# Three of the first eight bursts on bare weights, their sums masked at eviction; fewer ones loaded; the bias added ahead of the sums

## The reference, cut to what matters

```python
x: (128, 128, 512)   cond_8 = y: (128, 8)   weight: (8, 512, 512)   mask: (512, 512)   bias: (512,)
masked_w = weight * mask[None, :, :]
w_bot = einsum('bg,got->bot', y, masked_w)          # one 512x512 matrix per batch entry
out   = x + einsum('bnt,bot->bno', x, w_bot) + bias
```

## Time and profile before

| | |
|---|---|
| median of 3 runs | 605.12 us (604.96 to 605.41) |
| the profiled execution | 605.46 us, its span 603.7 us |
| PE busy | 592.5 us (98%) |
| DVE, ACT, POOL busy | 313.5, 142.0, 37.8 us |
| HBM traffic | 245 GB/s over the span, 406 GB/s in the slice from 15 to 30 us |

### The profile page before, as it was taken

One profiled execution on the slowest core, in us unless ns is written; L12 is line 12 of the kernel. 1 busy time (PEld: TensorE's weight loads), 2 busy tenths in 40 slices (PEclk: granted clock), 3 DMA queues, 4 the chain that ended last, 5 costly groups with the idle time before them and its releaser, 6 DMA issues.

```text
span 603.7 us, 14813 instructions
## 1 busy us (share of the span) xinstructions
PE 592.5 (98%) x6343; PEld 515.9 (85%) x6343; DVE 313.5 (52%) x524; ACT 142.0 (24%) x277; POOL 37.8 (6%) x34
## 2 busy tenths in 40 slices
PE   7899999999999999999999999999999999999998
PEld 6899988888888888888888888888888888888886
DVE  3565535455555555464465465555555555654342
ACT  4443322222222222222222222222222222220000
POOL 3430000000000113221000000000000000000000
PEclk9999999999999999999999999999999999999999
DMA  9976656686776899998766756766767766777952
GB/s 325 406 294 184 207 180 208 219 249 217 239 246 214 290 332 354 343 337 288 238 225 224 250 204 239 249 210 231 246 216 230 234 234 228 227 244 242 298 158 87
DMA packets 61089, 148.59 MB, mean 246 GB/s; under 512 B 6880, under 2 KB 9696, under 8 KB 61024
## 3 DMA queue, kind: packets, MB, share of 16 engines
q1 hardware_dynamic: 40176, 113.00, 57.3%
q10 hardware_dynamic: 20848, 34.64, 15.2%
HBM read 114.07 MB, written 33.55 MB: 245 GB/s over the span
## 4 chain that ended last, share of the span: by engine, by line
PE 95%; DMA 2%; DVE 1%; issue 1%; ACTq 0%; ACT 0%; DVEq 0%
PE ps L438 75%; PE ps L415 20%; DMA bias_sb<-in_bias 1%; DMA xs<-in_mask 1%; DVE wbot L321 0%; DVE staged L335 0%; PE ps L398 0%; ACTq L268 0%; DVE staged L349 0%; ACT wbot L263 0%; DVE wm L189 0%; DVE staged L354 0%; ACTq L277 0%; DVEq L161 0%; DVEq L346 0%
## 5 line engine op out<-in xcount | busy, mean ns | idle before, releaser
L438 PE MATMUL ps<-wbot,xs 128*128 128x256 f32 (+1 forms) x2176 | 459.3, 370 | 4.4 <-DVE wbot L321 3.7
L438 PEld LDWEIGHTS ps<-wbot,xs 128*128 128x128 f32 x2176 | 389.7, 190 | 59.2 <-issue 6.3
L321 DVE COPY wbot<-ps 128x512 f32<-128x512 f32 (+1 forms) x272 | 164.1, 649 | 183.8 <-PE ps L438 174.6
L263 ACT ACTIVATE wbot<-ps 128x512 f32<-128x512 f32 (+1 forms) x276 | 140.7, 568 | 400.7 <-PE ps L415 198.1
L415 PEld LDWEIGHTS ps<-y_sb,wm 32*128 32x128 f32 x4096 | 124.9, 190 | 21.7 <-issue 20.6
L415 PE MATMUL ps<-y_sb,wm 32*128 32x128 f32 x4096 | 137.5, 280 | 2.5 <-DVE wm L189 2.0
L349 DVE TENSOR_TENSOR staged<-ps,staged 128x512 f32<-128x512 f32 x111 | 76.3, 687 | 79.8 <-PE ps L438 79.8
L335 DVE TENSOR_TENSOR staged<-staged,bias_sb 128x512 f32<-128x512 f32 x112 | 76.4, 682 | 0.0
L189 POOL TENSOR_TENSOR wm<-wm,mask_sb 128x512 f32<-128x512 f32 x16 | 20.0, 1270 | 216.3 <-DMA mask_sb<-in_mask 216.3
L349 DVE TENSOR_TENSOR staged<-ps,bias_sb 128x256 f32<-128x256 f32 (+1 forms) x24 | 12.2, 510 | 15.5 <-PE ps L438 11.0
L189 POOL TENSOR_TENSOR wm<-wm,xs 128x512 f32<-128x512 f32 x14 | 17.6, 1274 | 21.7 <-DMA xs<-in_mask 21.4
(11 more groups left out here) (1 smaller groups left out, 0.1 us busy)
## 6 DMA issues: line engine op xcount, KB each, us to landing
xs<-in_x SPq DMA_DIRECT2D x128, 512.0 KB, 3.9
out<-staged ACTq DMA_DIRECT2D x119, 256.0 KB, 4.7
staged<-in_xn SPq DMA_DIRECT2D x112, 256.0 KB, 4.3
wm<-in_w SPq DMA_DIRECT2D x12, 512.0 KB, 6.4
mask_sb<-in_mask SPq DMA_DIRECT2D x8, 512.0 KB, 6.5
out<-staged ACTq DMA_DIRECT2D x18, 128.0 KB, 4.2
wm<-in_w SPq DMA_DIRECT2D x8, 256.0 KB, 6.8
xs<-in_mask SPq DMA_DIRECT2D x4, 512.0 KB, 13.4
```

The lines of the kernel that those rows point to most:

```text
L263: eng.activation(tile_place(b, j, first, end), tile_sums(b, j, first, end), ACT.Copy).then_inc(s_ev_a, 1)
L321: eng.tensor_copy(tile_place(b, j, first, end), tile_sums(b, j, first, end)).then_inc(s_ev_v, 1)
L438: ins = eng.matmul(bank[:, at_h:at_h + width], xs[:, n % XRING, h, k, :], at, start=(k == 0), stop=(k == KT - 1))
```

## The change

Bursts 0, 2 and 4 (`BARE`) are run on the weights as they come, without mask. VectorE evicts all four strips of them and multiplies by the mask on the way, from a transposed mask `mask_t` (204 KB with a small identity `one_sb`, loaded into the place of mask 0). GpSimd then adds the identity to their sums in `wbot` (`add_one`, one 128x512 instruction for each). Bursts 1, 3 and 5 are evicted by ScalarE alone. `AHEAD` loses 1, 3 and 5. GpSimd multiplies all masks, in the order 1, 3, add_one(0), 5, add_one(2), 6, 7, add_one(4), 8 to 15, and last 0, 2, 4, whose masks are loaded late, behind x 7 and x 9; the later windows need them. `load_x(2)` now also waits for the three add_one. Mask 1 moves to ScalarE's queue. `eye_sb` and `ones_sb` become one tile, blanked by GpSimd and filled by four DMAs of 9 KB that bring only its 16 used partitions. In VectorE's loop `add_bias_to_x(m + 2)` moves ahead of `add_sums(m)`.

```diff
-AHEAD = {1, 3, 5, 7, 8, 10, 12, 14}
+AHEAD = {7, 8, 10, 12, 14}
+BARE = (0, 2, 4)
+MASKED = tuple(_c for _c in range(CS) if _c not in BARE) + BARE
 def on_vector(b, j):
-    return j == 3 or j == 1 and b >= BY_VECTOR
+    if b < BARE[-1] + 2:
+        return b in BARE
+    return j % 2 == 1
...
         def masked(eng, s, c):
-            if s == 0 and c < BY_VECTOR:
-                eng.wait_ge(s_mul_v, c + 1)
-            else:
-                eng.wait_ge(s_mul_p, s * CS + c + 1 - BY_VECTOR)
+            eng.wait_ge(s_mul, len(MASKED) + c + 1 if s else MASKED.index(c) + 1)
...
-                elif c:
+                elif c > 1 and c not in BARE:
                     eng.dma_start(first_mask[:, c:c + count, :], mask[s, :, c:c + count, :]).then_inc(s_mask[c], 16)
             def load_x(n):
...
                     masked(eng, 0, n * 2 - 3)
+                    if n == 2:
+                        eng.wait_ge(s_one, len(BARE))
...
-            for n in range(7, XRING):
-                load_x(n)
+            load_x(7)
+            load_late(0)
+            load_late(1)
+            load_x(8)
+            load_x(9)
+            load_late(2)
...
-            eng.dma_start(first_mask[:, 0, :], mask[0, :, 0, :]).then_inc(s_mask[0], 16)
-            eng.dma_start(eye_sb[:, :, :].rearrange("p v t -> p (v t)").bitcast(fp32), eye).then_inc(s_eye, 16)
-            eng.dma_start(ones_sb[:, :].bitcast(fp32), ones).then_inc(s_eye, 16)
+            eng.dma_start(first_mask[:, 0, 0:KT * GB * BT + BT // 2], mask_t).then_inc(s_mask_t, 16)
+            eng.dma_start(first_mask[:, 1, :], mask[0, :, 1, :]).then_inc(s_mask[1], 16)
+            eng.wait_ge(s_blank, 1)
+            for j in range(TILES):
+                eng.dma_start(eye_sb[j * TR:j * TR + TO, :, :].rearrange("p v t -> p (v t)").bitcast(fp32),
+                              eye[j]).then_inc(s_eye, 16)
...
+            def add_one(b):
+                at = sums[:, b, :, 0, :, :]
+                o = BARE.index(b) * CO
+                eng.wait_ge(s_ev_v, DONE[b, TILES - 1, GROUPS])
+                eng.tensor_tensor(at, at, one_sb[:, o:o + CO].unsqueeze(1).unsqueeze(1).to_broadcast([P, GROUPS, GB, CO]),
+                                  ALU.add).then_inc(s_one, 1)
+
+            for c in MASKED:
+                multiply_mask(eng, 0, c).then_inc(s_mul, 1)
+                if c - 3 in BARE:
+                    add_one(c - 3)
...
+                        if b in BARE:
+                            o = BARE.index(b) * CO + j * TO
+                            by = mask_t_sb[:, :, o:o + TO].unsqueeze(2).to_broadcast([P, KT * GB, GROUPS, TO])
+                            if b == BARE[0]:
+                                eng.wait_ge(s_mask_t, 16)
+                            eng.tensor_tensor(tile_place(b, j, first, end), tile_sums(b, j, first, end), by,
+                                              ALU.mult).then_inc(s_ev_v, 1)
...
-                add_sums(m)
                 if OWN_X <= m + 2 <= LAST:
                     add_bias_to_x(m + 2)
+                add_sums(m)
```

More of the change, by code:

```diff
@@ L99, with cond_resid_kernel @@
 LOAD_W_AT = {LAST_UNIT - GROUPS + 14 + _c: _c for _c in range(0, CS, 2)}
-def cond_resid_kernel(nc: bass.Bass, x, xn, w, mask, bias, yblk, eye, ones, out):
+def cond_resid_kernel(nc: bass.Bass, x, xn, w, mask, mask_t, bias, yblk, eye, out):
     fp32 = mybir.dt.float32
@@ L141, in cond_resid_kernel @@
         s_mask = [sem(f"s_mask{i}") for i in range(CS)]
-        s_mul_v = sem("s_mul_v")
-        s_mul_p = sem("s_mul_p")
+        s_mul = sem("s_mul")
+        s_mask_t = sem("s_mask_t")
+        s_one = sem("s_one")
+        s_late = [sem(f"s_late{c}") for c in BARE]
         s_x = [sem(f"s_x{i}") for i in range(XRING)]
@@ L186, in multiply_mask @@
             eng.wait_ge(s_w[lead], 16 * (s + 1))
-            eng.wait_ge(s_mask[lead], 16 * (s + 1))
-            by = first_mask[:, c, :] if s == 0 else mask_sb[:, c % MASKN, :]
+            if s == 0 and c in BARE:
+                eng.wait_ge(s_late[BARE.index(c)], 16)
+                eng.wait_ge(s_s1, (c + 1) * TILES)
+                by = mask_sb[:, BARE.index(c) % MASKN, :]
+            else:
+                eng.wait_ge(s_mask[lead], 16 * (1 if lead in BARE else s + 1))
+                by = first_mask[:, c, :] if s == 0 else mask_sb[:, c % MASKN, :]
             return eng.tensor_tensor(wm[:, c, :], wm[:, c, :], by, ALU.mult)
@@ L211, in load_w @@
                 if s:
-                    if c >= MASKN:
-                        masked(eng, s, c - 1)
+                    masked(eng, *((s, c - 1) if c >= MASKN else (s - 1, MASKED[-1])))
                     eng.dma_start(mask_sb[:, 0:count, :], mask[s, :, c:c + count, :]).then_inc(s_mask[c], 16)
-                elif c:
+                elif c > 1 and c not in BARE:
                     eng.dma_start(first_mask[:, c:c + count, :], mask[s, :, c:c + count, :]).then_inc(s_mask[c], 16)
@@ L222, in load_x, with load_late @@
                     masked(eng, 0, n * 2 - 3)
+                    if n == 2:
+                        eng.wait_ge(s_one, len(BARE))
                 u, g = divmod(n, GROUPS)
                 eng.dma_start(xs[:, n % XRING, :, :, :], x[u % WINDOWS * GROUPS + g]).then_inc(s_x[n % XRING], 16)
+            def load_late(i):
+                if i >= MASKN:
+                    masked(eng, 0, BARE[i - MASKN])
+                eng.dma_start(mask_sb[:, i % MASKN, :], mask[0, :, BARE[i], :]).then_inc(s_late[i], 16)
             def load_xn(m):
@@ L309, in _ @@
         def _(eng):
-            for s in range(SLICES):
+            eng.memset(eye_sb[:, :, :].rearrange("p v t -> p (v t)").bitcast(fp32), 0.0).then_inc(s_blank, 1)
+            def add_one(b):
[8 more added lines that the diff above has]
+                    add_one(c - 3)
+            for s in range(1, SLICES):
                 for c in range(CS):
-                    if s or c >= BY_VECTOR:
-                        multiply_mask(eng, s, c).then_inc(s_mul_p, 1)
+                    multiply_mask(eng, s, c).then_inc(s_mul, 1)
         @block.vector
@@ L320, in evict @@
                         tile_ready(eng, b, j)
-                        eng.tensor_copy(tile_place(b, j, first, end), tile_sums(b, j, first, end)).then_inc(s_ev_v, 1)
+                        if b in BARE:
[5 more added lines that the diff above has]
+                                              ALU.mult).then_inc(s_ev_v, 1)
+                        else:
+                            eng.tensor_copy(tile_place(b, j, first, end),
+                                            tile_sums(b, j, first, end)).then_inc(s_ev_v, 1)
             def bias_of(m):
@@ L356, in _ @@
             eng.memset(staged[:, 0, :], 0.0).then_inc(s_zeros, 1)
-            for c in range(BY_VECTOR):
-                multiply_mask(eng, 0, c).then_inc(s_mul_v, 1)
             for b in range(HALF):
@@ L386, in burst @@
                 bank = [ps[BANK_OF[b, j] % BANKS] for j in range(TILES)]
-                ahead, behind = b in AHEAD, u == 0 and b not in AHEAD
+                ahead, behind = b in AHEAD, u == 0 and b not in AHEAD and b not in BARE
                 others = [k for k in range(KT) if k != own]
                 def add_x():
-                    if b == 0:
-                        eng.wait_ge(s_eye, 32)
+                    if b == 1:
+                        eng.wait_ge(s_eye, 16 * TILES)
                     for j in range(TILES):
@@ L406, in burst @@
                     eng.wait_ge(s_y_rest, 16)
-                if win == 0:
+                if b in BARE:
+                    eng.wait_ge(s_w[c], 16)
+                elif win == 0 or u == 1 and c in BARE:
                     masked(eng, s, c)
@@ L430, in piece @@
                         tile_evicted(eng, u * CS + end - 1, j, g + EARLY)
+                if m == 0:
+                    eng.wait_ge(s_one, len(BARE))
                 bank = room((m, None))
@@ L479 @@
     }
+    bare = [c * CO + o for c in BARE for o in range(CO)]
+    mask_t = np.broadcast_to(np.asarray(L0_cond_mask)[bare].reshape(len(bare), KT, 1, P).transpose(3, 1, 2, 0),
+                             (P, KT, GB, len(bare))).reshape(P, KT * GB * len(bare))
+    one = np.zeros((P, len(bare)), np.uint16)
+    for i, o in enumerate(bare):
+        one[o, i] = 0x3F80
+    a["mask_t"] = np.concatenate([mask_t, one.view(np.float32)], axis=1)
     blocks = np.zeros((WINDOWS, CO, NG, GB, GROUPS, TO), y.dtype)
@@ L484 @@
     a["yblk"] = blocks.reshape(WINDOWS, P, W * TO)
-    eye = np.zeros((TILES, TR, P // CO, P), np.uint16)
-    ones = np.zeros((TILES, TR, W, TO), np.uint16)
+    eye = np.zeros((TILES, TO, P // CO + 1, P), np.uint16)
     for j in range(TILES):
         for o in range(TO):
-            ones[j, o, :, o] = 0x3F80
+            eye[j, o, P // CO, o::TO] = 0x3F80
             for v in range(P // CO):
                 eye[j, o, v, v * CO + j * TO + o] = 0x3F80
-    a["eye"] = eye.reshape(P, P // CO * P).view(np.float32)
```

(4 more changed lines are left out.)

9 lines of the change are left out of this document (6 added, 3 removed).

## The result

The changed kernel takes 608.54 us (median of 4 runs, 608.08 to 609.14) against 605.26 us (604.96 to 605.87) for the kernel before, measured beside it: ratio 1.0048, 95% interval 1.0036 to 1.0060. It is slower by 3.3 us, outside the forecast range of 603.2 to 606.5 us. The profiled execution took 608.08 us, its span 606.3 us: 2.6 us more than before.

The account below looks back on a forecast made before the run. The prediction took the start, and the order of two VectorE instructions, as what was at stake. Its terms, +0.55 - 0.9 - 0.2 = -0.55 us, gave 604.9 us profiled, 604.5 as a median, range 603.2 to 606.5.

Parts of the forecast that it names:

- What bounds the kernel: Whole kernel: PE is busy 592.5 of 603.7 us; the start and the order of two VectorE instructions are at stake.
- The clock: At the start: PE's rise to full speed comes by burst 1, after a 1.9 us pause.
- rival B: At the start: slow clock until 12.6 us or later, piece 0 at 22.3, +1.4 us: 605.9 us; chance 0.22.
- main case: Whole kernel: full clock by burst 1, piece 0 at 20.9 us, 603.8 to 605.2 us in all; chance 0.50.
- The eviction chains: Start: four evictions take 2.5 us on VectorE, 2.2 on ScalarE; piece 0 starts at 20.9, 0.55 us later.
- GpSimd: Start: mask multiplies and add_one take 1.27 us each, hidden for bursts 6 and 7; add_one(4) ends at 18.6.
- rival C: Start: add_one priced at 3.5 us; piece 0 +2.5 us, late masks 10-11 +1.4 more: 608.4 us; chance 0.13.
- SP's queue: load_x(2) waits until 18.6, DMA idles 1.3 us, masks 10-11 land after 26.3: no cost, 1.2 us in hand.
- The bias: Bursts 8 and 9: the bias comes at 24 us, a gain of 0.9 us (0.2 at 26.5).
- The unit starts: Unit boundaries: the bias addition ahead of the sums lies in idle time, gaining 0.2 us, at most 0.8.
- xn: VectorE's loop: an xn landing late could hold add_sums, but VectorE has slack, so no cost.
- The sum: Whole kernel: +0.55 - 0.9 - 0.2 = -0.55 us from 605.46, so 604.9 profiled and 604.5 as a median.

Follow-up runs that it names:

- nine: The changed kernel run again, unchanged: 608.25 us, ratio 1.0039 to the kernel before.
- Four: The changed kernel with eight 128x512 matmuls on zeros between bursts 0 and 1: 605.92 us, ratio 1.0011 to the kernel before.
- five: The changed kernel with eight filling matmuls and its first six bursts evicted by both engines, ScalarE's strips of bursts 0, 2, 4 unmasked: 605.85 us.
- eleven: The changed kernel with eight filling matmuls, first six bursts evicted by both engines (some strips unmasked), bias ahead only outside 215 to 345 us: 603.78 us.
- One: The kernel before with only add_bias_to_x(m + 2) moved ahead of add_sums(m): 605.99 us, ratio 1.0015 to the kernel before.
- two: The changed kernel with the old order, add_sums(m) ahead of add_bias_to_x(m + 2): 606.73 us, ratio 1.0019 to the kernel before.

## Why the prediction was wrong, point by point

**What bounds the kernel** was read rightly: the start and the order of two VectorE instructions are where the time moved.

**The clock: the first step that failed.** "I take the rise to come by burst 1" was right and not enough. The clock did rise in burst 0 (which takes 1.71 us for 2.09), and fell again near 9.1, when burst 1 had just begun behind 2.55 us of pause. In its price that is rival B, which put piece 0 at 22.3; it came at 22.18 (22.73 in nine). B's reason was another one, that the clock doesn't rise at all until 12.6. Four shows the cost by keeping PE busy: 12.35 us from burst 1 to piece 0 instead of 13.37, and piece 0 at 20.75, where the main case said 20.9. The prediction named a pause of 1.9 us ahead of burst 1 and gave it no cost in the main case; it counted only how much unbroken work raises the clock, and not that the pause which GpSimd's 1.27 us and mask 1's landing leave could take it away again. The Trainium skill, "TensorE: Matmul & The Clock Gate", Part 1, which the prediction draws on, names that half too: an idle stretch brings the throttle back. The rows of after agree, with the granted clock down at 9.1 behind the pause.

**The eviction chains** were right. VectorE's multiply takes 684 ns (0.69 forecast), four take 2.48 (2.5), ScalarE's four 2.06 (2.2). With the clock up, the path from burst 1 to piece 0 is 12.35 us, as the list gave it (20.9 - 8.6 = 12.3), and halving the evictions shortens it by 1.8 (10.52 in five and eleven). Bare bursts start early and gain nothing, since burst 1 waits for its mask and each later one for a whole engine's four evictions.

**GpSimd** was right in size: add_one takes 1.14 us (1.27), so rival C fell. But with bursts 2 and 4 late by the clock, the additions are late: the third ends at 19.8, not 18.6.

**SP's queue: the second step that failed, in size.** "So this costs nothing, and 1.2 us are in hand." Load x 2 went out at 19.93, and the DMA ran at 68 GB/s from 17.5 to 21.5. Masks 10-11 were there at 29.6 where 26.3 was forecast: 1.3 of the 3.3 us because x 2 went out later than at 18.6, and 2.0 because they came 9.7 us after that issue and not 7.7. The gap in the transfers that the prediction put at 1.3 us was the undersized term. This cost 0.6 us by piece 7. That it cost anything is a consequence of the late additions, and so of the slow clock: four has the same gap (x 2 at 17.97, masks 10-11 at 27.32, 9.4 us later) and loses nothing by it.

**The bias** was right: -0.99 us measured, -0.9 forecast. The 2.98 us of the forecast left out the first identity matmuls, which its 2.07 has in; like for like it is 3.05 - 2.07 = 0.98. The bias itself came at 25.7 and not at 24. **The unit starts**: -0.8 measured, -0.2 taken and 0.8 the bound; the 0.11 us of each boundary (the idle before the first piece falls from 0.31 or 0.36 to 0.19) was the upper value.

**xn: the third step that failed, and the largest.** "An xn landing late could now hold add_sums: VectorE has slack, no cost." VectorE's slack over the whole kernel is beside the point: its sums free the PSUM bank that the next burst needs, and they now stand behind a wait for a transfer (PE waits for them at 244.00). The order of before waited for nothing (no idle time at L335), for it asked for `xn` one piece later. The step rested on no row for the landing of `xn`; in the stretch of the slice-1 loads it is up to 9.2 us. One and two show the net price of the order alone: +0.7 us in the kernel before, 1.2 to 1.8 us in the changed one.

**The sum** by those terms in the profiled executions: +1.80 (forecast +0.55), -0.99 (-0.9), +0.60 (0), -0.8 (-0.2), +2.0 (0) = 2.6 us. The medians lie 3.3 us apart in the first timing, and 2.6 us in nine (608.25 against 605.69): the changed kernel spreads more. One and two add up to 0.7 + 1.2 = 1.9 us, less than that; that late starts lengthen the waits for `xn` would explain it, but no run isolates it, and it stays open. The measured 608.5 us is also what rival C was priced at (608.4); that is chance, since C's cause, a slow `add_one`, didn't occur.

## What to carry to other kernels

Before an instruction is moved ahead of one that frees a buffer, look at what it waits for in the worst stretch of the kernel, not at its median (here 9.2 us against 4.3): an instruction that waits for a transfer blocks everything behind it in its engine's order. A matmul burst that is started early is worth little if the next one isn't ready: it only opens a pause, and here the pause cost the clock; close it with cheap work, or leave the burst where it was. When a data load stops being the bound, ask whether each engine's chain of evictions is shorter than what the load had hidden.

## What the runs showed of the hardware

- GpSimd's addition over 16 stretches of 32 fp32 columns with a broadcast bf16 input took 1143 ns, less than its 1267 ns for two plain fp32 inputs of 512 columns.
- The third transfer of ScalarE's queue, 256 KB issued at 1.65 us, landed after 5.3 to 7.3 us in the profiles of four kernels that issue it alike; a burst that hangs on one early transfer inherits that spread.
